# A changed opening: x tiles before context tiles, V in slots 5 to 12, keys in slots 4 and 6, rope tables in four banks

## What is computed

```python
x = x + xattn(layernorm(x), ctx, ctx, pos, mask)
x = x + layernorm(x) @ dequantised(kernel) + bias

# xattn
q, k, v = query @ Wq, ctx @ Wk, ctx @ Wv
q = q * cos[pos] + rotate_half(q) * sin[pos]      # the same for k
scores = q @ k.T / sqrt(128), masked where mask == 0
out = softmax(scores) @ v @ Wo
# the feed-forward weight is rounded to mxfp4 in blocks of 32
```

## Time and profile before

| | us |
|---|---|
| median of 3 runs | 1170.5 (1167.52 to 1610.54) |
| the profiled execution, its own time | 1170.62 |
| its span in the profile | 1168.8 |

### The profile page before, as it was taken

The page is one execution under the profiler, slowest core; times in us unless marked ns, Lnnn a source line. Parts: engine busy times, 40 slices in busy tenths (PEclk is TensorE's granted clock), DMA queues, the critical chain, the costliest instruction groups (busy, mean ns, idle before and its releaser), DMA issues.

```text
span 1168.8 us, 19640 instructions
## 1 busy us (share of the span) xinstructions
PE 1138.0 (97%) x6320; PEld 974.6 (83%) x6320; DVE 813.2 (70%) x1744; ACT 762.7 (65%) x2297; POOL 637.1 (55%) x524
## 2 busy tenths in 40 slices
PE   5899999999999999999999999999999999999998
PEld 4778888888888888888788788888888888888865
DVE  7667777777777777678787756656666666656677
ACT  5476766667666766778665557676766666765652
POOL 6665654455553664579665455544654455454332
PEclk9999999999999999999999999999999999999999
DMA  7230301111010111234112121110200111110001
GB/s 229 64 97 10 90 15 32 54 44 67 24 59 24 55 49 37 62 97 130 51 50 82 65 81 54 32 51 19 82 10 28 55 37 54 28 55 1 19 10 64
DMA packets 51604, 63.47 MB, mean 54 GB/s; under 512 B 8752, under 2 KB 27312, under 8 KB 51504
## 3 DMA queue, kind: packets, MB, share of 16 engines
q1 hardware_dynamic: 49008, 59.07, 16.4%
q0 software_dynamic: 768, 2.10, 0.6%
q10 hardware_dynamic: 1728, 1.05, 0.3%
HBM read 58.01 MB, written 4.19 MB: 53 GB/s over the span
## 4 chain that ended last, share of the span: by engine, by line
PE 86%; DVE 4%; issue 4%; POOL 3%; ACT 2%; DMA 0%; POOLq 0%; DVEq 0%; ACTq 0%
PE proj L415 14%; PE proj L416 14%; PE proj L417 14%; PE pS L504 8%; PE pO L547 8%; PE pO L548 8%; PE pO L549 8%; PE pV L534 2%; PE pV L535 2%; PE pT L517 2%; PE pO L557 2%; PE pO L560 1%; PE proj L429 1%; POOL acc L1001 1%; PE proj L460 1%
## 5 line engine op out<-in xcount | busy, mean ns | idle before, releaser
L698 ACT CAST PS<-pT 64x256 fp32r<-64x256 f32 x256 | 93.8, 366 | 286.4 <-PE pV L535 281.1
L1007 POOL TENSOR_TENSOR t<-t,SIN 128x512 f32<-128x512 f32 x128 | 164.7, 1287 | 202.2 <-ACT t L669 196.7
L415 PE MATMUL proj<-XH,QH 128*128 128x512 f32 x512 | 202.0, 395 | 2.5 <-DVE XL L757 2.1
L416 PE MATMUL proj<-XL,QH 128*128 128x512 f32 x512 | 200.0, 391 | 0.0
L417 PE MATMUL proj<-XH,QL 128*128 128x512 f32 x512 | 199.9, 390 | 0.0
L547 PE MATMUL pO<-OH,AH 128*128 128x512 f32 x448 | 178.4, 398 | 0.0
L548 PE MATMUL pO<-OL,AH 128*128 128x512 f32 x448 | 175.6, 392 | 0.0
L549 PE MATMUL pO<-OH,AL 128*128 128x512 f32 x448 | 174.7, 390 | 0.0
L1012 POOL TENSOR_TENSOR qT<-qT,t 128x512 f32<-128x512 f32 x128 | 165.2, 1290 | 10.0
L779 DVE TENSOR_TENSOR qT<-proj,COS 128x512 f32<-128x512 f32 x128 | 88.4, 690 | 100.2 <-PE proj L417 59.8
L705 ACT ACTIVATE pS<-pS,tiny 128x64 f32<-128x64 f32 x512 | 142.9, 279 | 15.6 <-DVE tiny L919 11.3
(11 more groups left out here) (136 smaller groups left out, 2547.3 us busy)
## 6 DMA issues: line engine op xcount, KB each, us to landing
OR<-wo SPq DMA_DIRECT2D x64, 256.0 KB, 3.0
QR<-wq SPq DMA_DIRECT2D x63, 256.0 KB, 2.6
acc<-x SPq DMA_DIRECT2D x16, 256.0 KB, 4.3
KR<-wk SPq DMA_DIRECT2D x16, 256.0 KB
out<-acc SPq DMA_DIRECT2D x16, 256.0 KB, 2.0
CR<-ctxT SPq DMA_DIRECT2D x15, 256.0 KB, 4.3
UR<-wv SPq DMA_DIRECT2D x14, 256.0 KB, 3.6
rawx<-x SPq DMA_DIRECT2D x8, 256.0 KB, 3.0
```

The source lines that it names most:

```text
L415: pe.matmul(dst, lh, rh, start=k == 0, stop=False)
L416: pe.matmul(dst, lh, rl, start=False, stop=False)
L1007: pool.tensor_tensor(t2[:, :], t2[:, :], SIN[:, 512 * (s % 2):512 * (s % 2) + 512], ALU.mult).then_inc(g_qs, 1)
```

## The change

Four things move, all in the first 14 slots:

- Loads: SyncE and ScalarE load x0 to x3 first, then the query weights; wk, wv and most context tiles come later (`weight_stream`). ScalarE's queue issues only x1 and x3. The wo tiles of the first group are spread over slots 5 to 8; masks are handled two slots later.
- V of the first eight context tiles moves from the prologue and slots 0 to 6 to slots 5 to 12, one a slot.
- The first two key projections move from slots 1 and 5 to slots 4 and 6 (`k_step`).
- Rope tiles 4 to 7 use the four banks too, and wait only for the copies of the tile four before.

VectorE's, ScalarE's and GpSimd's prologues are put in the matching order; x4 to x7 are copied (`x_high`) at the head of a slot and normalised ahead of times_cos.

```diff
 def v_tile(n):
 
-    if -1 <= n < 7:
-        return divmod(n + 1, 4)
+    if 5 <= n < 13:
+        return divmod(n - 5, 4)
     s, t = (n - 3) // 4, (n - 3) % 4
     return (s, t) if 2 <= s < STEPS and (s // 2) % 2 == 0 else None
...
+def k_step(n):
+
+    if n in (4, 6):
+        return (n - 4) // 2
+    return n // 4 if 8 <= n < PAIRS and n % 4 == 1 else None
...
-    out = [(-1, "v", 0, 0), (-1, "v", 1, 0), (-1, "q", 0, 0), (-1, "c", 0, 0), (-1, "c", 0, 1), (0, "c", 0, 2),
-           (0, "c", 0, 3), (0, "k", 0, 0), (0, "q", 0, 1), (1, "q", 0, 2), (1, "c", 1, 0), (2, "q", 0, 3),
-           (2, "c", 1, 1), (2, "c", 1, 2), (3, "c", 1, 3)]
+    out = [(-1, "q", 0, 0), (-1, "q", 0, 1), (0, "q", 0, 2), (0, "c", 0, 0), (0, "q", 0, 3), (0, "c", 0, 1),
+           (2, "k", 0, 0), (3, "v", 0, 0), (3, "v", 1, 0), (3, "c", 0, 2), (4, "c", 0, 3), (5, "c", 1, 0),
+           (5, "c", 1, 1), (6, "c", 1, 2), (6, "c", 1, 3)]
     for G in range(HALVES * GROUPS):
         if G:
             out += [(8 * G - 3 + h, "q", G, h) for h in range(4)]
-            out.append((8 * G - 2, "k", G, 0))
+            out.append((8 * G - 2 if G > 1 else 8, "k", G, 0))
             if G % 2 == 0:
-                out += [(8 * G - 4, "v", G, 0), (8 * G + 2, "v", G + 1, 0)]
-        out += [(8 * G + 3, "o", G, 0), (8 * G + 4, "o", G, 1), (8 * G + 8, "o", G, 2), (8 * G + 8, "o", G, 3)]
+                out += [(8 * G - 4 if G > 2 else 14, "v", G, 0), (8 * G + 2, "v", G + 1, 0)]
+        out += [((8 * G + 3, 8 * G + 4, 8 * G + 8, 8 * G + 8)[h] if G else 5 + h, "o", G, h) for h in range(4)]
...
-            where = (pS, pT, pO, pV.rearrange("p b t -> p (b t)"))[T] if T < 4 else pS
+            where = (pS, pT, pO, pV.rearrange("p b t -> p (b t)"))[T % 4]
...
-            return n - 1 if 0 <= n - 1 < 8 else n - (HALF - 2) + 8 if 0 <= n - (HALF - 2) < 8 else None
+            return n - 3 if 0 <= n - 3 < 8 else n - (HALF - 2) + 8 if 0 <= n - (HALF - 2) < 8 else None
...
+            load_x(0)
+            sp.dma_start(ident[:, :], eye).then_inc(d_eye, 16)
+            load_x(2)
             load_stream(-1)
+            load_x(4)
+            load_stream(0)
+            for T in range(5, 8):
+                load_x(T)
             for n in range(FIRST, END):
-                load_stream(n)
+                if n:
+                    load_stream(n)
...
-                    pe.wait_ge(a_cs, 2 * T)
+                    pe.wait_ge(a_cs, 2 * T - 6)
...
-                if n == 4:
-                    project_v(*v_tile(n))
...
-                if 0 <= n < PAIRS and n % 4 == 1:
-                    project_k(n // 4)
-                if v_tile(n) and n != 4:
+                if k_step(n) is not None:
+                    project_k(k_step(n))
+                if v_tile(n):
...
-            for i in range(4):
-                _, _, raw, src, loaded, _ = weight(*STREAM[i][1:])
-                act.dma_start(raw, src).then_inc(loaded, 16)
-            high(-1)
-            for T in range(4):
-                x_high(T)
+            for T in (1, 3):
+                act.dma_start(acc[:, T, :], x[T]).then_inc(d_x[T], 16)
+            x_high(0)
+            high([0])
+            x_high(1)
+            high([1])
+            x_high(2)
+            x_high(3)
...
+                if n - 1 in X_AT and X_AT[n - 1] < 8:
+                    x_high(X_AT[n - 1])
...
+            normalise("x", 1)
             statistics("x", 3)
-            normalise("x", 1)
             normalise("x", 2)
             x_low(0)
             normalise("x", 3)
-            x_low(1)
-            low(3)
-            x_low(2)
-            x_low(3)
-            low(4)
+            for T in range(1, 4):
+                x_low(T)
...
+                lows = [i for i in streamed(n) if lo_on_dve(i)]
+                if n == 0:
+                    low(lows.pop(0))
+                if n in X_AT and (X_AT[n] < 8 or X_AT[n] % 4 == 3):
                     normalise("x", X_AT[n])
+                for i in lows:
+                    low(i)
...
-            gather(0)
-            low(0)
-            inverse("x", 0)
-            low(1)
-            inverse("x", 1)
-            inverse("x", 2)
-            gather(1)
-            low(2)
+            for T in range(3):
+                gather(T)
+                inverse("x", T)
             inverse("x", 3)
-            for T in range(2, 5):
-                gather(T)
+            low(PLACE["q", 0, 0])
+            low(PLACE["q", 0, 1])
+            gather(3)
+            gather(4)
+            inverse("x", 4)
+            low(PLACE["q", 0, 2])
+            gather(5)
+            low(PLACE["q", 0, 3])
+            gather(6)
...
+                if n in X_AT and n:
...
-                if n < 3:
-                    gather(n + 5)
+                if n == 2:
+                    gather(7)
```

More of the change, by code:

```diff
@@ L116, in bank_uses @@
 def bank_uses():
-    out = [("x", T) for T in range(4)] + [("v", 0)]
+    out = [("x", T) for T in range(4)]
     for n in range(FIRST, END):
-        if n == 4:
-            out.append(("v", v_count(*v_tile(n)) - 1))
         if 0 <= n < PAIRS:
@@ L129, in bank_uses @@
             out.append(("r", ROPE_AT[n]))
-        if 0 <= n < PAIRS and n % 4 == 1:
-            out.append(("k", n // 4))
-        if v_tile(n) and n != 4:
+        if k_step(n) is not None:
+            out.append(("k", k_step(n)))
+        if v_tile(n):
             out.append(("v", v_count(*v_tile(n)) - 1))
@@ L334, in load_stream @@
                 for i in streamed(n):
-                    if i < 4:
-                        continue
                     _, kind, a, b = STREAM[i]
@@ L354, in load_stream, with load_x @@
                     sp.dma_start(raw, src).then_inc(loaded, 16)
+            def load_x(T):
+                sp.dma_start(acc[:, T, :], x[T]).then_inc(d_x[T], 16)
             def fk_rows(i):
@@ L398, in _ @@
                     sp.dma_start(bias[:, :], fbias).then_inc(d_bias, 16)
-                if n in (0, 1):
-                    for j in (2 * n + 4, 2 * n + 5):
-                        sp.dma_start(acc[:, j, :], x[j]).then_inc(d_x[j], 16)
                 j = n - HALF - 7
@@ L565, in _ @@
                 turn_x(T)
-            project_v(0, 0)
             for n in range(FIRST, END):
                 m = n - 5
-                if n == 4:
-                    project_v(*v_tile(n))
                 if 0 <= n < PAIRS:
@@ L608, in _, with high @@
         def _(act):
-            def high(n):
-                for i in streamed(n):
+            def high(some):
+                for i in some:
                     hi, _, raw, _, loaded, k = weight(*STREAM[i][1:])
@@ L683, in _ @@
                                  proj[:, BANK["w", i], 0:256].rearrange("p (k t) -> p k t", k=2)).then_inc(a_w4, 1)
-                if n - 1 in X_AT:
+                if n - 1 in X_AT and X_AT[n - 1] >= 8:
                     x_high(X_AT[n - 1])
@@ L687, in _ @@
                     f_high(FFN_AT[n - 1])
-                high(n)
+                high(streamed(n))
                 if n == 0:
@@ L922, in _ @@
                     ffn_add(FFN_AT[n - 2])
-                if n in X_AT and X_AT[n] % 4 != 3:
+                if n in X_AT and X_AT[n] >= 8 and X_AT[n] % 4 != 3:
                     normalise("x", X_AT[n])
@@ L955, in _ @@
                     ffn_add(FFN_AT[n - 1])
-                if 0 <= n < PAIRS and n % 4 == 1:
-                    s = n // 4
+                if k_step(n) is not None:
+                    s = k_step(n)
                     dve.wait_ge(e_kp, s + 1)
@@ L1034, in _ @@
                     add_bias(FFN_AT[n])
-                if n in X_AT:
+                if n in X_AT and n:
                     inverse("x", X_AT[n])
@@ L1041, in _ @@
                     rotate_q(n - 1)
-                for i in streamed(n):
+                for i in streamed(n) if n else ():
                     if not lo_on_dve(i):
@@ L1055, in _ @@
                     gather(ROPE_AT[n] + 2)
-                if 0 <= n < PAIRS and n % 4 == 1:
-                    rotate_k(n // 4)
+                if k_step(n) is not None:
+                    rotate_k(k_step(n))
 def rope_table():
```

## The result

| | us |
|---|---|
| changed kernel, median of 6 runs | 1174.59 (1173.83 to 1175.54) |
| before, median of its 6 runs | 1169.82 |
| ratio to before, 95% interval | 1.0049 [1.0037, 1.0061] |
| profiled execution / span | 1175.08 / 1173.3 |

The change makes the kernel 0.5% slower, about 5.7 us by the ratio and 4.5 us by the two spans: clear of noise, and far inside 2%. One of the six executions of the kernel before took 1610.54 us; the ratio leaves it out. The forecast was 1173.

A forecast was written before the change was run, and what follows sets the result against it. TensorE, busy 1138 of 1168.8 us, bounds the kernel, leaving the opening where it waits. Terms +1.6 + 1.0 + 1.9 - 1.8 = +2.7 us gave 1173.3, stated as 1173; range 1164 to 1180.

The forecast's parts named there:

- Start and slots 0 to 3: Opening up to projection 4: projection 0 starts near 16.0, projection 4 at 40.9; +1.6 us, between -0.5 and +2.3.
- the 39.3: Start of projection 4 in us without loss or gain, with the 11.3 us of work formerly ahead of it taken off.
- Slot 5: scores(0) waits for key projection 0, now behind projection 4: 0.8 us, up to 1.4 with queued lows; +1.0 taken.
- Slot 6: Key projection 1 waits for the lows of c6 and c7, streamed in its own slot: 0.7 to 3.2 us, +1.9 taken.
- the rival of slot 6: Key projection 1 waits 3.2 us, then runs at 1.2 GHz: +6.5 to +8.5 us, 1178; chance 0.17.
- Slots 7 to 9: Old TensorE waits of 1.2 and 0.6 us, for a softmax and a rotation, vanish: -1.8 us (0 to -1.8).
- Cover: Slots 0 to 3: V work filling TensorE is gone, so the chain of VectorE, ScalarE and GpSimd stands bare.
- The lock or a sharing: VectorE and GpSimd ports: exclusive lock costs a normalisation up to 1.3 us; mere sharing slows it to 1.1, sum +1.3.

The follow-up runs named there:

- The first experiment: Changed kernel with context tiles c4 to c7 of the second key step streamed one slot earlier; ratio to the kernel before 1.0013, median 1169.99 us.
- the better version: Changed kernel with context tiles a slot earlier, last rope gather in the prologue, and low(k0) behind the power of x7; ratio to before 0.9985, 1166.95 us.

## Why the prediction was right

It was right in direction and mechanism, and the result lies inside its range. Of the size, +2.7 us were forecast, and 4.5 (by the spans) to 5.7 (by the ratio) came: one term was too small, and a better start hid part of it.

*Start and slots 0 to 3.* Projection 0 was put at 16.0 and stands at 15.31. The estimate had low(q0) catch normalise x3 for its whole length; it caught it for part (0.94 us). Projection 0 itself was put at 2.74 + 1.6 us and took 5.26 to the start of the next work (15.31 to 20.57), slow from end to end, so that the early start was used up at projection 1 (21.8 foretold, 22.13 seen). The wait for x5 was put at 2.0 us and is 1.22, by the mechanism foretold. The gap before projection 4 was put at "some 7 us" and is 5.6, at the places foretold: rope tile landing (36.7 foretold, 36.04 seen), normalise x7, low(c2), times_cos, mask, XL. Step taken +1.6, measured +0.7, inside -0.5 to +2.3. With its collision normalise x7 was to end at 37.4 and ended at 36.3: GpSimd's chain ran some 0.7 us earlier. Part of the +0.7 is luck: the slow spell of projection 0 was 0.9 us longer than taken, and the earlier start and the earlier chain on GpSimd outweighed it. The lengths of 2.74 and 1.43 us are those of later projections and V tiles; from the rows that the prediction names (11 matmuls in 2.61 and in 1.38 us) they come to 2.85 and 1.51, which would put the 39.3 at 38.7. And the clock ahead of projection 4 does not quite cancel: the slow spell there cost 0.6 us more than before.

*Slot 5.* +1.0 taken, +1.4 measured: the upper of the two bounds, 0.8 and 1.4. low(c4) slipped in just ahead of rotate_k (49.97 against 50.08 us), which took 1.70 us instead of 1.29. That this is what set the wait was not tried.

*Slot 6.* This is the mis-sized term. Taken +1.9; measured 2.7 of waiting and 1.7 at the lower clock, +4.3. The wait is inside the bounds of 0.7 to 3.2. The clock was counted in the rival and not in the forecast, though the prediction itself had the row for it: 2.14 us of idle ahead of 50.64, with slow matmuls behind. The condition of that rival, lows that end more than about 2 us after TensorE arrives, came true, at 2.7 and not 3.2 us. The sum took the middle of the two bounds of the wait and nothing for the clock, although the long end of the wait could bring the slow spell with it. It need not: before, a wait of 2.92 us ahead of the transpose at 41.38 was followed by a projection at full pace (2.99 us from start to end). What decides between the two was not tried. The first experiment confirms both parts: without the wait the key projection takes 2.98 us. The outcome lies between the forecast and the rival of slot 6 (1178), nearer the forecast.

*Slots 7 to 9.* -1.8 taken, -2.2 measured; only 0.13 us of waiting is left.

*Cover.* The prediction said that V had filled TensorE and that without it the chain would stand bare. The run with V alone shows it: 7.2 us of work out, 0.4 us won. It also suggests that the rest of the change (x first, query weights first, later keys, four banks) is worth about 1.0065 - 1.0049 = 0.0016 of the time, nearly 2 us, though the two intervals overlap; the starts of projection 10, 94.35 and 92.57, say the same 1.8 us. Which of these parts brings that was not tried one by one, except the rope banks, which bring some 0.4 us by the trace.

*The lock or a sharing.* The normalisation beside a rotation half takes 1.49 us where sharing would have given about 1.1, and the run in which GpSimd waits brings x5 and x7 back to 0.55. The Trainium skill, SBUF — State Buffer, section "Who interferes with whom", has an exclusive lock for the length of an instruction. The rows agree with it in the main: the normalisation ends only after the rotation has (24.94 to 26.43, the rotation from 24.88 to 26.13). They differ in the length: it ends 0.30 us behind the rotation, not its whole 0.55.

## What to carry to other kernels

Work that fills the waits of a full engine in an opening is free there and costs its whole length where the engine is continuous; before moving it, compare the chain of the other engines with and without it, not the waits by name. Move the operands of a step at least a slot ahead of it: two subtractions in the slot of their use cost 4.2 us here, one slot earlier no wait is left. And price an added wait with and without a slow spell behind it: here 2.7 us of waiting cost 4.3, while a wait of 2.9 us before had no such spell behind it.

## What the runs showed of the hardware that was not expected

- A collision of VectorE with GpSimd works in both directions and through a series: low(c4) ahead of rotate_k made that 1.70 us long, and two CL beside rotate_q and the lows of wv took 3.42 us where two undisturbed ones take 1.29. Even the small mask operation (128x128, 0.21 us alone) took 0.68.
- Giving one side the right of way (GpSimd waiting until the normalisation was done) removed every collision that it was aimed at and none of the time: 1.0051 against 1.0049, and 0.9996 against 0.9985 on the better version.
- Nearly the same opening met slow spells of different length from kernel to kernel: projection 0 took between 4.36 and 5.46 us in the changed kernel and the seven built on it, though TensorE's order is the same up to there. What follows moves with it: from projection 0 to projection 4 the first experiment takes 1.1 us less than the changed kernel, from projection 1 on 0.3 less. So 1 us between two profiles of one opening is no finding, and landmarks are better counted from projection to projection.
- The spell of projection 0 does not show in the granted clock, which is 1.00 from 14 to 22 us in the changed kernel, while its matmuls stand 0.43 us apart. The slow pace there is read from the matmuls.
